# A recurrent layer step put in another order on four engines, and the next attention's first work moved inside it

## What is computed

```python
def _bitlinear(x, w, nw):          # rows rounded to 8 bits, weights to -1, 0, 1
    xn = _rmsnorm(x, nw)
    return jnp.einsum('bld,ed->ble', act_quant(xn), weight_quant(w))
i = _bitlinear(hidden_states, w_i, nw_i)
f = jax.nn.sigmoid(_bitlinear(hidden_states, w_f, nw_f))
g = _bitlinear(hidden_states, w_g, nw_g)
h = ft * h + (1.0 - ft) * it       # over the 1024 tokens, from h = 0
o = _rmsnorm(o, g_norm_w) * g * jax.nn.sigmoid(g)
return _bitlinear(o, w_o, nw_o)    # added to x
# then the cross attention (its queries from the normalised x, its keys and values from ctx_768)
q = split(x @ Wq + bq); k = split(y @ Wk + bk); v = split(y @ Wv + bv)
```

## Time and profile before

| | |
|---|---|
| median of 3 runs | 1433.38 us (1432.4 to 1435.71) |
| profiled execution, device time | 1429.83 us |
| its span, first to last instruction | 1428.1 us |
| mean granted TensorE clock | 0.954 of full speed |
| busy share of the span | PE 90%, DVE 71%, ACT 62%, POOL 32% |

### The profile page before, as it was taken

How to read it: one execution, slowest core, us unless ns; L and a number is a source line. 1 busy time by engine, 2 the same in 40 slices (tenths; PEclk the granted TensorE clock), 3 DMA queues, 4 the chain that set the end, 5 groups by cost and what they waited for, 6 DMA issues and landing times. The chain is left out here.

```text
span 1428.1 us, 27677 instructions
## 1 busy us (share of the span) xinstructions
PE 1290.6 (90%) x9691; PEld 1035.0 (72%) x9691; DVE 1011.2 (71%) x2014; ACT 881.6 (62%) x2215; POOL 457.0 (32%) x628
## 2 busy tenths in 40 slices
PE   5989999999699999989999866689987799999996
PEld 3534444436599999977888654588876799999995
DVE  4688877834666666556789687678866588888773
ACT  4427666674476666645121467478873688888873
POOL 5311222228443343326000256311101244444430
PEclk9979999999899999999999988699998799999998
DMA  4755333200000000003000310032204577777855
GB/s 91 212 99 146 60 46 47 47 1 5 30 2 2 1 2 2 1 25 102 1 0 1 77 22 1 23 71 48 50 2 137 172 231 232 230 233 232 232 151 186
DMA packets 97916, 116.15 MB, mean 81 GB/s; under 512 B 23549, under 2 KB 83187, under 8 KB 97779
## 3 DMA queue, kind: packets, MB, share of 16 engines
q1 hardware_dynamic: 88323, 99.83, 26.5%
q0 software_dynamic: 4416, 12.06, 2.7%
q10 hardware_dynamic: 5040, 2.49, 0.7%
HBM read 88.47 MB, written 16.55 MB: 74 GB/s over the span
## 5 line engine op out<-in xcount | busy, mean ns | idle before, releaser
L827 ACT ACTIVATE sa_probs<-ps 128x512 f32<-128x512 f32 (+1 forms) x304 | 154.4, 579 | 86.8 <-PE ps L780 85.7
L851 DVE TENSOR_REDUCE sa_top<-ps 128x2 f32<-128x1024 f32 (+3 forms) x160 | 171.9, 1114 | 39.8 <-PE ps L756 25.7
L2736 PE MATMUL ps<-me_h,me_w_parts 128*128 128x256 f32 x1104 | 141.2, 289 | 4.3 <-issue 2.5
L2736 PEld LDWEIGHTS ps<-me_h,me_w_parts 128*128 128x128 f32 x1104 | 137.7, 194 | 5.8 <-issue 2.7
L2750 PE MATMUL ps<-me_w_parts,me_mid 128*128 128x256 f32 x1104 | 136.6, 284 | 0.0
L2750 PEld LDWEIGHTS ps<-me_w_parts,me_mid 128*128 128x128 f32 x1104 | 132.7, 189 | 0.0
L3244 ACT ACTIVATE room<-ps,cx_top 128x154 f32<-128x154 f32 x256 | 96.4, 390 | 35.6 <-DVE cx_top L3293 35.0
L2801 ACT ACTIVATE me_full<-ps,me_b 128x256 f32<-128x256 f32 x184 | 95.3, 518 | 35.7 <-PE ps L2736 35.7
L2817 DVE TENSOR_TENSOR me_w_parts<-me_chunk,me_w_parts 128x1024 fp32r<-128x1024 f32 x92 | 110.4, 1222 | 9.3 <-ACT me_w_parts L2777 6.6
L2847 DVE TENSOR_TENSOR me_mid<-me_full,me_mid 128x256 fp32r<-128x256 f32 x184 | 90.4, 510 | 35.6 <-ACT me_mid L2803 35.6
L3123 POOL TENSOR_TENSOR room<-room 128x512 f32<-128x512 f32 x64 | 67.0, 1048 | 142.3 <-DVE room L3301 142.2
(11 more groups left out here) (466 smaller groups left out, 3362.9 us busy)
## 6 DMA issues: line engine op xcount, KB each, us to landing
me_chunk<-in_L_ffn_W_dram SPq DMA_DIRECT2D x92, 512.0 KB, 4.5
sa_k<-scr_k SPq DMA_DIRECT2D x48, 128.0 KB, 4.3
sa_q<-scr_q SPq DMA_DIRECT2D x96, 64.0 KB, 4.4
cn_qd<-cn_qh SPq DMA_DIRECT2D x60, 64.0 KB, 2.0
scr_q<-room SPq DMA_DIRECT2D x6, 512.0 KB, 4.8
scr_k<-room SPq DMA_DIRECT2D x6, 512.0 KB, 5.2
me_b<-in_L_ffn_b_dram SPq DMA_DIRECT2D x23, 128.0 KB, 3.8
x<-in_x_dram SPq DMA_DIRECT2D x4, 512.0 KB, 5.9
```

Source lines behind the costliest of these rows:

```text
L827: act.activation(probs[:, step % self.PROBS, h0:h0 + many, 0:w], src[:, :, 0:w], ACT.Exp, scale=DH ** -0.5).then_inc(exped.sem, 1)
L851: dve.tensor_reduce(top2[:, k % 2, k0 // 512, h0:h0 + many, sb % HBLK], src[:, :, 0:w], AX.X, ALU.max).then_inc(freed.sem, 1)
L2736: last = pe.matmul(ps[:, MID + n % 4, 0:RT], w[:, u % 2, 0, i, DM * k + P * b:DM * k + P * b + P], h[:, u % 2, j, k, :], start=(m == 0), s ...
```

## The change

Only the order of instructions changes, and the step in which each hangs; a few semaphores' counts follow. POOL does `keep`, `rounds`, `gated`, `zo` and the output rounding in this order. PE does `products` ahead of `scan_turn` and `turn_back`. ACT does `sq_h` behind `forget_t`. DVE does `gate`, `new`, `scan`, `u`, `top_o`, and `rows` with `scales` behind these. The keys and values come behind the products and sigmoids of step 0 rather than ahead of the loop. The splitting of the weights goes from the steps 15 to 17 to the steps 2 to 4; root and normalising are done for two tiles at a time in steps 16 to 21; the first queries come in steps 18 to 21 rather than 21 to 24; the bias product goes from step 19 to 24.

```diff
@@ POOL
-                nx.pool_keys(pool)
+                nx.pool_zero(pool)
...
                 for k in range(STEPS):
-                    if 0 <= k - 1 < NT:
-                        at(pool, "gate", k)
-                        pool.tensor_tensor(gate[:, (k - 1) % 4, :], gate[:, (k - 1) % 4, :], norm_g[:, :], ALU.mult
-                                           ).then_inc(s["gated"].sem, 1)
                     if k < NT:
                         at(pool, "forget", k + 1)
                         if k >= 2:
                             at(pool, "new", k - 1)
                         pool.tensor_scalar(keep[:, k % 2, :], forget[:, k % 2, :], -1.0, 1.0, ALU.mult, ALU.add
                                            ).then_inc(s["keep"].sem, 1)
+                    if k == 0:
+                        nx.pool_keys(pool)
+                    if KNOWN <= k + 3 < NT:
+                        rounds(k + 3)
+                    if k < NT:
+                        at(pool, "gate", k + 1)
+                        pool.tensor_tensor(gate[:, k % 4, :], gate[:, k % 4, :], norm_g[:, :], ALU.mult
+                                           ).then_inc(s["gated"].sem, 1)
                     if 0 <= k - 2 < NT:
                         t = k - 2
                         at(pool, "u", t + 1)
                         pool.tensor_tensor(zo[:, t, :], u[:, t % 2, :], norm_o[:, :], ALU.mult).then_inc(s["zo"].sem, 1)
-                    if KNOWN <= k + 3 < NT:
-                        rounds(k + 3)
@@ PE
                 turn(0)
-                nx.tensor_keys(pe)
                 for k in range(STEPS):
                     if k + 1 < STEPS:
                         turn(k + 1)
                     nx.tensor_wait(pe, k)
+                    products(k)
+                    if k == 0:
+                        nx.tensor_keys(pe)
+                    if 0 <= k - 1 < NT:
+                        scan_turn(k - 1)
                     if 0 <= k - 2 < NT:
                         turn_back(k - 2)
-                    products(k)
-                    if 0 <= k - 1 < NT:
-                        scan_turn(k - 1)
                     nx.tensor_step(pe, k)
@@ ACT: the square of step k - 2 (L1907 to L1913) goes behind the copy forget_t (L1933)
-                nx.scalar_keys(act)
-                nx.scalar_values(act)
...
+                    if k == 0:
+                        nx.scalar_keys(act)
+                        nx.scalar_values(act)
@@ DVE: gate and new (L2037 to L2048), scan (L2028 to L2037), u and top_o (L2015 to L2027), then:
+                    if k in ROW_STEPS:
+                        t = KNOWN + ROW_STEPS.index(k)
+                        rows(t)
+                        if t % 2:
+                            scales(t - 1)
@@ pool_step
-        if k == 15:
+        if k == 2:
             self.wait(pool, "q_in", 16)
...
-        if k == 16:
+        if k == 3:
             self.wait(pool, "o_high", 1)
...
-        if k == 17:
+        if k == 4:
             self.wait(pool, "q_high", 1)
...
-        if k in (19, 20):
-            self.wait(pool, "inverted", 1)
-            for t in (2 * k - 38, 2 * k - 37):
+        if k in (17, 21):
+            self.wait(pool, "inverted", (k - 13) // 4)
+            for t in ((k - 17) // 2, (k - 15) // 2):
@@ tensor_step
-        if k == 19:
+        if k == 24:
             self.wait(pe, "o_in", 32)
...
-        if k == 21:
+        if k == 18:
             self.turn_x(pe, 0)
-        if k in (22, 23):
-            self.queries(pe, 0, k - 22)
+        if k in (19, 20):
+            self.queries(pe, 0, k - 19)
@@ scalar_step (the copies of wo and wq go from 15 and 16 to 2 and 3)
-        if k == 18:
-            self.wait(act, "shifted", 1)
-            act.activation(self.sd[:, 0:4], self.ve[:, 0:4], ACT.Sqrt).then_inc(s["rooted"].sem, 1)
+        if k in (16, 18):
+            a = slice(k - 16, k - 14)
+            self.wait(act, "shifted", (k - 14) // 2)
+            act.activation(self.sd[:, a], self.ve[:, a], ACT.Sqrt).then_inc(s["rooted"].sem, 1)
...
@@ vector_step: the same split for ve (16, 18) and rstd (17, 19); low_x 22 to 19, low_q 24 to 21
```

More of the change, by code:

```diff
@@ L1934, in _ @@
                                        ).then_inc(s["forget_t"].sem, 1)
+                    if k == 0:
+                        nx.scalar_keys(act)
+                        nx.scalar_values(act)
+                    if 0 <= k - 2 < NT:
+                        t = k - 2
+                        at(act, "back", t + 1)
+                        if t >= 1:
+                            at(act, "sq_h", t)
+                        act.activation(junk[:, 0, 0:D], back_out(t), ACT.Square, accum_out=sum_h[:, t:t + 1]
+                                       ).then_inc(s["sq_h"].sem, 1)
                     if 0 <= k - 3 < NT:
@@ L2009, in _ @@
                 for k in range(STEPS):
-                    if k in ROW_STEPS:
-                        t = KNOWN + ROW_STEPS.index(k)
-                        rows(t)
-                        if t % 2:
-                            scales(t - 1)
+                    if k < NT:
+                        at(dve, "sig_g", k + 1)
+                        if k >= 4:
+                            at(dve, "u", k - 3)
+                        dve.scalar_tensor_tensor(gate[:, k % 4, :], ps[:, GO, 0:D], unit[:, k, 2:3], sig_g[:, k % 2, :],
+                                                 ALU.mult, ALU.mult).then_inc(s["gate"].sem, 1)
+                        at(dve, "keep", k + 1)
+                        if k >= 2:
+                            at(dve, "s_turned", k - 1)
+                        dve.scalar_tensor_tensor(new[:, k % 2, :], ps[:, FI + k % 2, D:2 * D], unit[:, k, 0:1],
+                                                 keep[:, k % 2, :], ALU.mult, ALU.mult).then_inc(s["new"].sem, 1)
+                    if 0 <= k - 1 < NT:
+                        t = k - 1
+                        at(dve, "forget_t", t + 1)
+                        if t:
+                            at(dve, "scanned", KD * t)
+                        for d in range(KD):
+                            first = 0.0 if t % ST == 0 else h[:, d, P * t - 1:P * t]
+                            dve.tensor_tensor_scan(h[:, d, P * t:P * t + P], forget_t[:, t % 2, P * d:P * d + P],
+                                                   ps[:, SCAN + t % 2, KD * P + P * d:KD * P + P * d + P],
+                                                   first, ALU.mult, ALU.add).then_inc(s["scanned"].sem, 1)
                     if 0 <= k - 2 < NT:
```

63 lines of the change are left out of this document (19 added, 44 removed).

## The result

The changed kernel is slower by a little. Its median is 1434.82 us (1431.66 to 1440.46) against 1432.32 us (1426.49 to 1439.09) for the kernel before, with 20 runs of each; the ratio is 1.0027, with an interval of 1.0015 to 1.0040, so 2.1 to 5.7 us on 1432. The profiled execution took 1433.27 us, with a span of 1431.5 against 1428.1.

What follows compares the result with a forecast made beforehand. The prediction took DVE to bound steps with rows, and a chain of scan, products, sigmoids and forget_t the others. Its terms summed to +3.9 us on the median of 1433.38, so 1437.3 us, range 1430.8 to 1441.0.

Steps and rivals of the forecast that it cites:

- Start: Block's start: rows of tile 8 now stands behind the first scan, uncovered, with DVE idle before it; +2.2 us.
- Steps 3, 6 and 9: Steps without rows: the chain is cut, gate to gate falls from 3.89 to 2.2 us; -4.9 us in all.
- Keep late in steps 7 and 10: POOL's keep comes late after the shortened steps, so DVE's new waits 0.7 us in steps 7 and 10; +1.4 us.
- Weight split: POOL's split in step 3, which has no rows, makes keep of tile 4 late for DVE; +2.0 us.
- Square root of step 10: ACT's table load after the root delays the sigmoids of step 11, so DVE idles ahead of its gate; +1.7 us.
- Rounds at step 11: Rounds of tile 14 wait for DVE's last scales, holding POOL and ACT; stall 3.0 us in step 12, net +1.35.
- Steps 13 to 15: Late steps without rows: the chain through POOL sets 3.4 us a step against 3.89; -1.5 us.
- Step 16: Square root moved here from step 18: table load and root stand ahead of ACT's squares, delaying the last u; +1.1 us.
- End: Block's end: bias product uncovered at step 24, +1.65 us, less 1.1 for PE's wait for xn; net +0.5.
- the faster one: Rival: POOL not late and PE at 2.4 GHz in the query part; 1430.2 us, chance 0.13.
- POOL is not late: Rival: keep follows u in under 1.05 us, so POOL's delays go; +3.9 becomes 0, 1433.4 us, chance 0.20.
- The heavier case: Rival: PE falls to 1.2 GHz after the stalls and bounds steps 12 to 15; +6.6 us, 1440.0 us, chance 0.20.

Runs made afterwards that it cites:

- the experiment: The changed kernel with DVE's out scales of step 10 ahead of that step's rows; block 111.4 us against 112.0.
- the combination: Changed kernel with rows one step earlier, splits at 1, 3, 4, step 10's out scales before rows, add before scan, bias at 19; 1427.64 us, 0.9965 of before.
- the bias kernel: The changed kernel with the bias product at step 19 in place of step 24; block 112.4 us against 112.0.

## Why the prediction came out as it did

The forecast of 1437.3 on a median of 1433.38 was +3.9 us; +2.1 to +5.7 was measured, and the block ended at 917, as the sum said. In the trace the block took 4.2 more and the span 3.4. Most terms of the sum hold, one fell, and one has the right size for a wrong reason. That the sum came within 0.3 of the block's 4.2 is in part luck: against the 1.2 that was missed in steps 13 to 15 stand six terms that came out a little lower than forecast, and the last two terms lie in C, where kernels with the same code differ by up to 1.9. The signs that the prediction had named for being right are all there. The measure below is how far the end of a DVE step lies behind the same step's end before, each from its block's start, and by how much a step changed that.

- **Start,** +2.2 forecast: +1.9 at the end of step 1. Its `rows` is bare as said, and moving it into the idle time brought 1.4 to 1.5 back.
- **Steps 3, 6 and 9,** -4.9 forecast: -1.2, -2.0 and -1.5, so -4.7. The gates were 2.46, 2.19 and 2.27 apart, where 2.2 was forecast.
- **Keep late in steps 7 and 10,** +1.4 forecast: +0.7 and +0.4. The waits are 0.50 and 0.29 rather than 0.7. From the start of `u` to the end of `keep` it took 1.59 (842.69 to 844.28) and 1.58, where 1.75 was estimated.
- **Weight split,** +2.0 forecast: +1.9 in step 4, and 1.1 to 1.7 came back when it was moved.
- **Square root of step 10,** +1.7 forecast: +1.4, with 1.59 us of wait in the trace, and 1.6 back in the experiment. The load is 1.28 at 862.30, and the sigmoid starts at 863.60, 0.02 behind its end. The Trainium skill (ScalarE: Activation LUTs, What ACT_TABLE_LOAD costs) adds a drain of 1380 ns to the load; here too no row shows it.
- **Rounds at step 11,** +1.35 forecast: +1.2. ACT's and POOL's waits of 4.13 and 5.09 are the stall, and of the two ACT's is the one that holds the gate, which the prediction had as its lower bound (2.5, and 2.40 measured). With the 0.38 that `new` of tile 12 still waited for POOL the stall is 2.8, where 3.0 was forecast.
- **Steps 13 to 15,** -1.5 forecast: -0.3. This is the step that failed. The prediction took the chain through POOL, 3.4 a step, as what sets the time, and the gates are 4.20 and 3.96 apart. It had looked for the wait of the product on `gate(k-1)`, but not on the output product in front of it, which waits for DVE's add of the step before. The add was last in DVE's step before, too, but the gate came late in the next step. The change put the gate first there, so that add, product, sigmoid and gate lie in one chain. Moving the add shows it: a step then took 3.42 on average, near the 3.4 that the prediction had for the chain through POOL.
- **Step 16,** +1.1 forecast: +1.5 in steps 16 and 17. The size fits and the cause is wrong. Without the root in that step, the waits of 1.00 and 1.08 were 1.62 and 1.29; with the root there and the add moved, the first was gone and the second 0.61. So most of both is the same chain as in steps 13 to 15: PE's output product waits for DVE's `x` there (2.49 at 886.40 and 2.05 at 889.70 in the changed kernel), and `turn_back` and the squares stand behind it. The load of 1.28 stands in a gap, as it did before: the squares of the last tile begin at 890.75, and `turn_back` has only just ended then, at 890.71.
- **End,** +0.5 forecast: +0.3, which is less than the scatter there, so the term is not confirmed by it. The bare bias took 1.91 at a clock of 0.50, where 1.65, at 0.62, was taken from the trace before. What it cost, 2.3, depends on the queries, which ran at the high clock only right behind it; so it and the gain of the earlier queries are not two terms that add up.

Of the rivals, the faster one would have had the bias and the queries run at the high clock; they had 0.50 and 0.58. (The trace has twelve query products, not the 24 that the prediction counts.) Moving the bias back, right ahead of the queries, gave the queries that clock. "POOL is not late" had its point at 1.05 us from `u` to `keep`; with 1.59 it was late, in step 7 by 0.50, and in step 4, behind the split, by 1.72. The heavier case came in half: the granted clock of the 20 us from 865 fell to 0.76 from 0.91, but in steps 13 to 15 four products took 0.60 us (878.48, 882.44), where two take 0.58 at the lower clock (889.70), so PE's pace didn't set those steps. Its waiting for DVE did.

## What to carry to other kernels

When an order is turned round on all engines at once, go through every wait of the instruction that is put first, and of those that stand ahead of it on the engine that feeds it: the chain that was missed ran through a neighbour in PE's list, not through the data. Put side work into the steps where the bound engine is already full or idle for another reason, not into those that have just been made short. And move stalls away one by one: five small moves turned a loss of 0.27% into a gain of 0.35%, while the order of PE and ACT alone cost 0.43%.

## What the chip showed besides

**The clock of the block behind.** That block's instructions are the same in all kernels, and its length fell into two groups: 168.6 to 169.5 and 171.5 to 172.3. They differ early. The stretch from 8 to 12 us behind its start, first in the kernel before, then in the changed one (columns as in the earlier trace rows):

```profile
921.04:925.04 4.00, 4.00 (x30) 4.00 (x29) 1.88 (x4) 2.46 (x8) 1.23 (x2) 0.81 0.00 0
```

```profile
924.97:928.97 4.00, 4.00 (x33) 4.00 (x31) 2.15 (x5) 2.73 (x8) 1.23 (x2) 0.88 0.00 0
```

And the same stretch in the combination and in the bias kernel:

```profile
916.29:920.29 4.00, 4.00 (x23) 4.00 (x22) 1.07 (x3) 2.25 (x7) 1.22 (x2) 0.58 0.00 0
```

```profile
927.89:931.89 4.00, 4.00 (x22) 4.00 (x21) 1.05 (x3) 2.33 (x8) 1.23 (x2) 0.54 0.00 0
```

PE is busy throughout, with 0.81 and 0.88 granted in the one group and 0.58 and 0.54 in the other, so at 1.2 GHz for nearly all of the stretch; ahead of it, at 0.50, PE had been busy 5.4 to 5.6 of 8 us in these four, and right behind it the clock is 1.00. So the rise from 1.2 to 2.4 GHz came at other times after nearly equal work. In all fourteen kernels this stretch and the length go together: 0.74 to 1.00 where the block is short, 0.54 to 0.63 where it is long. It isn't the price of a shorter block: the bias kernel has a block of 112.4 and still 172.3 behind it. What sets the moment stays open; it is worth 2 to 3 us here, as much as the change itself, and a block's length in one trace has to be judged apart from it.

**The same at the start.** The keys' and values' products of step 0, with the same code ahead of them, in the changed kernel and in the bias kernel:

```profile
809.43 2.44 PE L3488 MATMUL ps<-ct,cn_wk 96*128 96x308 f32 x8
811.71 1.89 PE L3494 MATMUL ps<-cn_wv,ct 96*128 96x256 f32 x8
```

```profile
811.99 4.32 PE L3488 MATMUL ps<-ct,cn_wk 96*128 96x308 f32 x8
816.10 3.29 PE L3494 MATMUL ps<-cn_wv,ct 96*128 96x256 f32 x8
```

4.32 and 3.29 rather than 2.44 and 1.89, so that the products end 3.2 us later in their block. 2.2 of these reach `gate` of tile 1, and A of the bias kernel is longer by that.

**DVE and POOL side by side.** `rows` took 1.39 in step 7 (above), beside POOL's `zo` and `keep`, and 0.99 in step 1, where POOL was idle when it began. POOL's `keep` took 1.11 in its turn:

```profile
845.94 0.73 POOL L1800 TENSOR_TENSOR hg_zo<-hg_u,hg_norm_o 128x256 f32<-128x256 f32 x1
...
846.65 1.11 POOL L1787 TENSOR_SCALAR room<-room 128x256 f32<-128x256 f32 x1
```

The Trainium skill (SBUF — State Buffer, 🔬 SBUF: two separate sides) has the pair of ports that DVE, with two inputs from SBUF, and GpSimd share as an exclusive lock for a whole instruction. The starts fit that to within 0.2 us: `rows` at 846.11 gets its 0.4 us extra while `zo` still runs, and `keep` at 846.65 is longer by 0.7, nearly as much as `rows` still has to run.
